# An earlier place for one batch's maxima in a latent-attention kernel: the order of work in the pair loop

## The chip, the cores and the metric

The kernel runs on one core of a Trainium2 chip. A core has five engines that run side by side: TensorE (PE in the profile; its weight loads are PEld), VectorE (DVE), ScalarE (ACT), GpSimd (POOL) and SyncE (SP, which here only issues DMAs). They wait for one another through semaphores. The metric is the device time of one execution in microseconds (us). The kernel before takes 814.68 us, the median of three runs (813.45 to 814.83).

## The reference

The reference is one block in three parts. The first is cross-attention of 64 latents on up to 1601 context rows plus the latents themselves, in each of 32 batches; it takes nearly all of the time. The second is a self-attention over the 64 latents, the third a quantised feed-forward layer.

```python
q = ln @ Wq                                   # ln: 64 latents x 128, per batch
k, v = split(concatenate((xn, ln)) @ Wkv)     # xn: context rows, normalised
sim = einsum('bhid,bhjd->bhij', q * scale, k) # 16 heads of 64
sim = where(mask_full, sim, -max)
attn = softmax(sim)
out = einsum('bhij,bhjd->bhid', attn, v) @ Wout
x = x + layernorm(out)
x = x + self_attention(layernorm(x))          # 16 heads of 8, with a slope bias
x = x + ffn(layernorm(x))                     # int8-like fake quantisation
```

The softmax needs, per head and latent, a maximum over all keys, which is subtracted before the exponential.

## The kernel before, in words

**Folding.** Keys are never formed. The queries are multiplied by the key weights, so that a "folded query" can be multiplied with the normalised context rows. Folded queries are made in three steps for a pair of batches, each in two halves: QP (latents times the query weights, lines 1376 to 1378), QC (times the key weights for the context, L1390) and QL (the same for the latents). Each has a high and a low 16-bit part: ACT copies the high part out of the bank, then DVE computes the low part (L1095 and L1903 for QP, L1103 and L1908 for QC, L1106 and L1912 for QL).

**Steps.** Here only the last 400 context rows of a batch differ in their mask and all earlier ones are masked out, so a flag that is read at run time picks the plan WINDOW, in which a batch has 8 steps. One body of the loop is one pair of batches: steps 0 to 7 belong to the even batch of pair i, steps 8 to 15 to the odd one. A step makes a bank of scores (L1435 to L1439), ACT turns them into two versions of the exponential (L1126 and L1117), POOL makes the low part (L861), and two steps later PE multiplies with the values (L1472). There are 16 bodies: body 0 and 1 written out, 2 to 14 in a loop of 13 turns, and body 15, which makes no queries.

**Jobs in between.** PE also makes the next work in advance, in "jobs" which alternate between two banks (jbank): T (transpose of the context rows, L1366), MAX (eight products of folded queries with all keys, only for the maximum, L1406 and L1407; DVE reduces each with L1916), MT (the eight maxima are negated by L1919, transposed by L1410, copied by L1923), QP, QC and QL. QP, T, MAX and MT take one bank each, QC and QL both banks. A job may start only when the bank it takes has been emptied, by DVE at last. The dictionary WINDOW gives each job its step: `ODD` the jobs of the odd batch of this body's pair, `NEXT` the queries of the next pair, `EVEN` the even batch of the next pair. At a step s, jobs at s are issued behind the step's scores and before its values, those at s+0.25 and s+0.5 behind the values, and the projections (L1552, L1569) and the self-attention of the pair before (`ST1`, `SC`, `ALIBI`, `SMAX`) behind those. Every engine walks the same table in its own program order. An instruction that waits holds all behind it on its engine.

**What the first MAX of the odd batch waits for.** The folded queries of QC are made one body ahead into a staging place (`arena`), and SP moves them to `qkc_h` and `qkc_l` by two DMAs (L636, L637). For the odd batch that move is the first thing that SP does in a body; it comes behind the DMA of line 668, which waits for DVE's reciprocal of the denominators (L1937, step 15 of the body before). The lines are these:

```python
if job.index == 0:
    pe.wait_ge(s_jobs_taken, plan.transposed_through(i, last, par))
    pe.wait_ge(s_lat_loaded[par], (b - par) * 8 + 16)
    if happened(b - 1):
        pe.wait_ge(s_qk_moved[par], (b - par) * 16)
```

`SMAX` is the reduction of the self-attention scores (L2028). POOL's subtraction (L929, `SHIFT`) waits for it.

Of the kernel before, what the change touches and what calls it, by code (L numbers as in the profile page):

```python
# [65 lines left out]
class Plan:  # L66
# [9 lines left out]
    def __init__(self, first, split, at):  # L76
# [19 lines left out]
        self.START = self.numbered(self.of_batch(0, at["START"]) + self.of_queries(at["START"]))  # L96
        odd, inner = self.of_batch(1, at["ODD"]), self.of_queries(at["NEXT"]) + self.of_batch(0, at["EVEN"])
        self.AHEAD = "AHEAD" in at
# [74 lines left out]
    START=dict(QP=[-3, -3], QC=[-2, -2], QL=[-1, -1], T=[0.5, 1.5, 2.5, 3.5], MAX=[11 + m // 3 + 0.5 * (m % 3 > 0) for m in range(32)], MT=23),  # L173
    ODD=dict(T=[0.5, 1.5, 2.5, 3.5], MAX=[11 + m // 3 + 0.5 * (m % 3 > 0) for m in range(32)], MT=23),
    NEXT=dict(QP=[5.5, 6.5], QC=[24.5, 26.5], QL=[33.5, 35.5]),
    EVEN=dict(T=[28.5, 29.5, 30.5, 31.5], MAX=[39 + m // 3 + 0.5 * (m % 3 > 0) for m in range(32)], MT=51), XV={8: (0, 3), 9: (3, 6), 10: (6, 9), 11: (9, 11), 12: (11, 13)},
    RDEN=(8, 8),
    MOVE=28, ST1=[10, 11, 14, 15], YN=[13, 17], XB=18, ST2=19, M0=21, P0=21, X1=22, X1B=23, M1=22, P1=23, XH=24, XHT=25, XHT_OUT=26, QKV=27, QKV_OUT=28,
    VBLK=29, KEXP=30, SC=34, ALIBI=[35, 37], SMAX=37, SHIFT=38, EXP=40, PT=[41, 43], PT_OUT=[42, 44],
# [1 line left out]
WINDOW = Plan(N - 400, ({0, 1, 2, 3, 4}, {0, 1, 2, 3, 4}), dict(  # L181
    STATS={4: (0, 4)}, AGGR=4, RSTD=5, XHAT=6, MASK=7,
    START=dict(QP=[-3, -3], QC=[-2, -2], QL=[-1, -1], T=[-2.5], MAX=[1, 1, 2, 2, 3, 3, 4, 4], MT=4.25),
    ODD=dict(T=[0], MAX=[2.5, 3, 3, 3.5, 4, 4, 4.5, 5], MT=6), AHEAD=[15.5],
    NEXT=dict(QP=[0, 0.5], QC=[1.5, 6.5], QL=[8.5, 9.5]),
    EVEN=dict(T=[7.5], MAX=[10.5, 11, 11, 11.5, 12, 12, 12.5, 13], MT=14.25), XV={2: (0, 4)},
    RDEN=(3, 7), MOVE=11, ST1=[4, 4, 6, 6], YN=[7, 7], XB=8, ST2=8, M0=9, P0=9, X1=10, X1B=20, M1=10, P1=11,
    XH=12, XHT=13, XHT_OUT=13, QKV=14, QKV_OUT=14, VBLK=15, KEXP=15.5, SC=17, ALIBI=[18, 20], SMAX=21, SHIFT=23, EXP=24,
    PT=[24, 25], PT_OUT=[24, 25], PV=26, CX=27, CXT=28, CXT_OUT=28, WO=29, X2=30, P2=31.5))


class Drain:
# [12 lines left out]
LAST_PAIR = Drain(True, dict(  # L205
    XB=1, DEN=0, ST1=[], RDEN=[1, 2], YN=[1, 2], ST2=[3, 4], M0=5, P0=5, X1=6, M1=6, P1=6, XH=7, XHT=7, XHT_OUT=7, QKV=8, QKV_OUT=8,
    KEXP=9, VBLK=10, SC=11, ALIBI=[12, 13], X1B=13, HALF_EXP=[12, 13], PT=[13, 14], PT_OUT=[14, 15],
# [5 lines left out]
def program(nc, x, ctx, mask, lnx_g, lnx_b, lnl_g, lnl_b, wq, wkv, wout, lno_g, lno_b,  # L213
            a_wq, a_bq, a_wk, a_bk, a_wv, a_bv, a_wo, a_bo, slopes, clip_x, clip_d, w_gate, w_up, w_down, out):
    es = ExitStack()
    with es:
# [1505 lines left out]
        def _(dve):  # L1722
# [234 lines left out]
            def second_norm(plan, p, s):  # L1957
                if s == plan.at["XH"]:
                    dve.wait_ge(s_rstd_a, p * 2 + 2)
                    centred(xh[:, :], x1[:, :], 1).then_inc(s_xh_ready, 1)  # L1960
# [231 lines left out]
```

## Time and profile before

| | |
|---|---|
| median of 3 runs | 814.68 us |
| the profiled execution | 815.53 us, span 813.8 us |
| PE busy | 749.8 us (92% of the span) |
| DVE busy | 597.5 us (73%) |
| ACT busy | 590.0 us (73%) |
| POOL busy | 543.7 us (67%) |
| mean granted clock of TensorE | 0.98 of full speed |

Times in the views are microseconds from the start of the span. In the views of single instructions a row gives the start, the time taken, the engine, the line and the tiles; several like instructions are merged (x3). Matmuls are pipelined: the difference of two starts tells what one costs, its own duration is longer. A bracket tells how long the engine sat idle and what ended it. The row `PEclk` of the page gives the granted clock of TensorE in tenths of full speed, in 40 slices.

### The profile page before, as it was taken

Reading aid. Unit: us, or ns where it says so; the run is one execution under the profiler, and the core shown is the slowest. Engines: PE = TensorE matmul, PEld = TensorE weight load, DVE = VectorE, ACT = ScalarE, POOL = GpSimd, SP = SyncE. Lnnn points to the kernel's source line nnn. Section 1 sums busy time; section 2 is a strip of 40 time slices with the busy share of each in tenths; the row PEclk is TensorE's granted clock in tenths of the full one; section 3 lists DMA queues with packets and bytes.
Section 4 is the critical chain, followed back from the end, with each engine's and each line's share of the span. In section 5 each row is a group of like instructions: output and inputs, shape, how many; then the busy total and the mean of one; then the engine's idle time right before and its main releaser. Section 6 shows DMA issues by size and latency. Waiting matters only on the chain.

```text
span 813.8 us, 22676 instructions
## 1 busy us (share of the span) xinstructions
PE 749.8 (92%) x7119; PEld 418.2 (51%) x7122; DVE 597.5 (73%) x1463; ACT 590.0 (73%) x1022; POOL 543.7 (67%) x712
## 2 busy tenths in 40 slices
PE   5698999999999999999999999999999999999666
PEld 3443544546555555555464555555555646455423
DVE  5877686676777777676767777776767676776677
ACT  5377777887878687878878686878787786866262
POOL 4366667676867768686868677686768686877122
PEclk9799999999999999999999999999999999999997
DMA  6302323121221202121211212021212122110001
GB/s 187 69 13 66 98 66 82 42 62 56 55 61 31 72 18 71 45 71 40 60 56 55 61 39 74 9 71 45 71 40 60 56 56 60 44 45 19 5 0 53
DMA packets 95822, 44.44 MB, mean 55 GB/s; under 512 B 66500, under 2 KB 87848, under 8 KB 95656
## 3 DMA queue, kind: packets, MB, share of 16 engines
q1 hardware_dynamic: 95728, 43.93, 19.5%
q8 instruction: 18, 0.29, 0.1%
q14 instruction: 20, 0.16, 0.1%
q10 hardware_dynamic: 56, 0.05, 0.0%
HBM read 24.20 MB, written 3.34 MB: 34 GB/s over the span
## 4 chain that ended last, share of the span: by engine, by line
PE 62%; DVE 17%; issue 11%; ACT 5%; POOL 3%; DVEq 1%; DMA 1%; ACTq 0%; POOLq 0%; SPq 0%
PE bank L1472 13%; PE bank L1552 7%; PE bank L1435 6%; PE bank L1439 5%; PE bank L1437 5%; PE bank L1390 4%; DVE mx L1916 3%; PE bank L1569 3%; DVE raw L1881 3%; PE bank L1407 3%; PE bank L1366 2%; PE bank L1587 2%; DVE qkl_l L1912 2%; PE bank L1406 2%; PE bank L1624 1%
## 5 line engine op out<-in xcount | busy, mean ns | idle before, releaser
L861 POOL TENSOR_TENSOR p<-arena,p 128x512 f16<-128x512 f32 x256 | 299.4, 1173 | 126.1 <-ACT arena L1117 124.6
L1126 ACT ACTIVATE p<-bank,maskbias 128x512 f16<-128x512 f32 x224 | 155.2, 693 | 103.5 <-PE bank L1439 101.4
L1472 PE MATMUL bank<-p,xv 128*128 128x512 f16 (+1 forms) x768 | 183.0, 381 | 1.3 <-POOL p L861 0.8
L1916 DVE TENSOR_REDUCE mx<-bank 128x1 f32<-128x464 f32 x256 | 154.0, 632 | 17.8 <-PE bank L1407 16.1
L1117 ACT ACTIVATE arena<-bank,maskbias 128x512 f32<-128x512 f32 x224 | 154.8, 691 | 0.0
L1472 PEld LDWEIGHTS bank<-p,xv 128*128 128x128 f16 (+1 forms) x768 | 58.5, 97 | 69.9 <-issue 23.0
L1912 DVE TENSOR_TENSOR qkl_l<-bank,qkl_h 128x512 f16<-128x512 f32 x64 | 41.1, 686 | 68.9 <-ACT qkl_h L1106 68.8
L1435 PE MATMUL bank<-qkc_h,xtT_h 128*128 128x512 f16 (+1 forms) x256 | 86.6, 389 | 0.0
L1437 PE MATMUL bank<-qkc_l,xtT_h 128*128 128x512 f16 (+1 forms) x256 | 85.0, 379 | 0.0
L1439 PE MATMUL bank<-qkc_h,xtT_l 128*128 128x512 f16 (+1 forms) x256 | 85.0, 379 | 0.0
L1407 PE MATMUL bank<-xtT_h,qkc_h 128*128 128x400 f16 x256 | 83.3, 338 | 0.0
L1881 DVE TENSOR_SCALAR raw<-raw,mv,rstd 128x128 f32<-128x128 f32 x128 | 72.7, 616 | 3.9 <-POOL rstd L870 2.0
L1908 DVE SCALAR_TENSOR_TENSOR arena<-bank,ident,arena 128x512 f16<-128x512 f32 x60 | 42.1, 743 | 27.6 <-ACT arena L1103 27.6
L1406 PEld LDWEIGHTS bank<-ltT,qkl_h 128*128 128x128 f16 x256 | 24.8, 97 | 71.0 <-DVE mx L1916 38.2
L1406 PE MATMUL bank<-ltT,qkl_h 128*128 128x64 f16 x256 | 50.9, 199 | 9.8 <-DVE mx L1916 5.1
L1552 PE MATMUL bank<-arena,wvF 128*64 128x128 f32 x960 | 59.0, 276 | 0.0
L1390 PE MATMUL bank<-arena,wk_h 64*128 64x128 f16 x1024 | 50.1, 217 | 5.3 <-DVE mT L1923 3.1
L1552 PEld LDWEIGHTS bank<-arena,wvF 128*64 128x64 f32 x960 | 51.8, 137 | 4.7 <-issue 3.3
L1390 PEld LDWEIGHTS bank<-arena,wk_h 64*128 64x128 f16 x1024 | 37.1, 94 | 32.8 <-DVE mT L1923 10.3
L1390 PE MATMUL bank<-arena,wk_l 64*128 64x128 f16 x512 | 46.1, 216 | 0.0
L1103 ACT ACTIVATE arena<-bank,ident 128x512 f16<-128x512 f32 x60 | 38.0, 685 | 8.3 <-PE bank L1390 8.3
L1903 DVE SCALAR_TENSOR_TENSOR arena<-bank,arena 128x512 f16<-128x512 f32 x32 | 22.0, 691 | 28.6 <-ACT arena L1095 28.6
(279 smaller groups left out, 1548.4 us busy)
## 6 DMA issues: line engine op xcount, KB each, us to landing
arena<-den_dram SPq DMA_DIRECT2D x62, 128.0 KB, 3.2
qkc_h<-arena SPq DMA_DIRECT2D x30, 256.0 KB, 2.4
qkc_l<-arena SPq DMA_DIRECT2D x30, 256.0 KB, 2.5
raw<-in_ctx SPq DMA_DIRECT2D x32, 192.0 KB, 2.4
lt<-lt_dram SPq DMA_DIRECT2D x60, 32.0 KB, 2.1
arena<-in_L_xattn_Wkv SPq DMA_DIRECT2D x1, 1024.0 KB, 7.5
raw<-in_ctx SPq DMA_DIRECT2D x64, 8.0 KB, 2.0
ltT_dram<-x_all SPq DMA_DIRECT2D x4, 256.0 KB, 3.0
```

Of the source, the lines that this page charges most:

```text
L861: g.tensor_tensor(p_halves[0:r, slot, 1, :], p_all[0:r, (plan.halves_made(0, k, t) - 1) % 2, :], p_halves[0:r, slot, 0, :], ALU.subtract). ...
L1117: a.activation(p_all[0:r, (plan.halves_made(0, k, t) - 1) % 2, :], sbank[t % SRING][0:r, :], ACT.Exp, bias=bias).then_inc(s_probs_ready, 1)
L1126: a.activation(p_halves[0:r, slot, 0, :], sbank[t % SRING][0:r, :], ACT.Exp, bias=bias)
L1390: op = mm(by_batch(both[odd])[:, :, to], w[rws, cl, c, :], q[rws, c, :].rearrange("p (k t) -> p k t", k=2), start=first, stop=final)
L1407: op = mm(bk[:, 0:rest], qkc_h[:, par, col], xtT_h[:, par, 512 * part:plan.KEYS], start=True, stop=True)
L1435: op = mm(dst, keys_h, q_h[:, col], start=True, stop=False)
L1437: op = mm(dst, keys_h, q_l[:, col], start=False, stop=False)
L1439: op = mm(dst, keys_l, q_h[:, col], start=False, stop=tile > 0)
L1472: op = mm(bk[:, :], halves_of[at, row, :], p_halves[at, slot, prob, :], start=tile < 2 and n == 0, stop=last and n == 2)
L1552: op = mm((one, two)[q // 2][E * odd:E * odd + E, (c % 4) * P:(c % 4) * P + P], wvF[:, cl, head:head + E], z[:, :, col:col + M], start=cl ...
L1881: op = v.tensor_scalar(raw[:, par, c, :], raw[:, par, c, :], mv[:, c, 0:1], rstd[:, c:c + 1], ALU.subtract, ALU.mult)
L1916: v.tensor_reduce(mx[:, hq_tile, part:part + 1], bk[:, 0:width], AX.X, ALU.max).then_inc(s_jobs_taken, 1)
```

## The change

Three entries of the table WINDOW change. No instruction is added or removed and none is computed otherwise; only the order on PE, ACT and DVE differs. On SP and POOL the order is the same.

```diff
-    ODD=dict(T=[0], MAX=[2.5, 3, 3, 3.5, 4, 4, 4.5, 5], MT=6), AHEAD=[15.5],
-    NEXT=dict(QP=[0, 0.5], QC=[1.5, 6.5], QL=[8.5, 9.5]),
+    ODD=dict(T=[0], MAX=[1, 1, 1.5, 1.5, 2.5, 2.5, 3, 3], MT=4.25), AHEAD=[15.5],
+    NEXT=dict(QP=[4.5, 5], QC=[5.5, 6.5], QL=[8.5, 9.5]),
-    ... ALIBI=[18, 20], SMAX=21, SHIFT=23, EXP=24,
+    ... ALIBI=[18, 20], SMAX=22, SHIFT=23, EXP=24,
```

On PE, in the turn of the loop, the odd batch's first two MAX jobs now stand directly behind the scores of step 1 (`qkc_h,xtT_h 64x512`), ahead of that step's values. These are rows of the difference:

```order
 L1435 MATMUL bank<-qkc_h,xtT_h 64x512 x2
 L1437 MATMUL bank<-qkc_l,xtT_h 64x512 x2
 L1439 MATMUL bank<-qkc_h,xtT_l 64x512 x2
+L1361 ISA
+L1395 REGISTER_ALU
+L1396 REGISTER_ALU
+L1398 REGISTER_ALU
+L1400 REGISTER_ALU
+L1406 MATMUL bank<-ltT,qkl_h 128x64
+L1407 MATMUL bank<-xtT_h,qkc_h 128x400
```

The ISA and REGISTER_ALU rows are the sequencer's: L1396 to L1400 compute the waits of the first MAX.

On ACT, in the turn of the loop of the kernel after, the two copies of QP and those of QC stand as follows, between the exponentials (L1126, L1117) of steps 4, 5 and 6; the words "waits" name the semaphores.

```order
185 L1117 ACTIVATE arena<-bank,maskbias 128x512 [waits p_lo]
186 L1090 ISA
187 L1095 ACTIVATE arena<-bank 128x512 [waits jobs_made]
188 L1119 REGISTER_ALU
189 L1126 ACTIVATE p<-bank,maskbias 128x512 [waits values_done,scores_ready]
190 L1116 REGISTER_ALU
191 L1117 ACTIVATE arena<-bank,maskbias 128x512 [waits p_lo]
192 L1090 REGISTER_ALU
193 L1095 ACTIVATE arena<-bank 128x512 [waits jobs_made]
194 L1090 REGISTER_ALU
195 L1100 ISA [waits jobs_made]
196 L1103 ACTIVATE arena<-bank,ident 128x2x256 [waits qk_moved1,qk_moved0]
```

The second copy of QP (row 193) follows both exponentials of step 5, and the copies of QC (from row 196) follow it at once. Before, the copies of QP stood at step 0 and those of QC at steps 1 and 6.

On DVE the self-attention maximum now stands behind the normalisation of the next context rows (L1881), and MT's copy (L1923) far ahead of both:

```order
-L1919 TENSOR_REDUCE negm<-mx 128x8
+L1879 REGISTER_ALU
+L1881 TENSOR_SCALAR raw<-raw,mv,rstd 128x128 x4
 L2027 ISA
 L2028 TENSOR_REDUCE smax<-arena 128x16
-L1895 REGISTER_ALU
-L1922 ISA
-L1923 CAST mT<-bank 8x128
-L1879 REGISTER_ALU
-L1881 TENSOR_SCALAR raw<-raw,mv,rstd 128x128 x4
```

## Rows read from the trace of the kernel before

**Rows 1.** The page: engines, granted clock by slices, chain of waits by engine.
```profile
PE 749.8 (92%) x7119; PEld 418.2 (51%) x7122; DVE 597.5 (73%) x1463; ACT 590.0 (73%) x1022; POOL 543.7 (67%) x712
PEclk9799999999999999999999999999999999999997
PE 62%; DVE 17%; issue 11%; ACT 5%; POOL 3%; DVEq 1%; DMA 1%; ACTq 0%; POOLq 0%; SPq 0%
```

**Rows 2.** Busy time by stretch: steps 0 to 7, then 8 to 15 of body 9.
```profile
core 0: us, PE busy (x) PEld busy (x) DVE busy (x) ACT busy (x) POOL busy (x), PEclk, DMA share, GB/s
438.94:461.34 22.40, 22.08 (x228) 12.17 (x228) 17.49 (x41) 15.81 (x27) 18.11 (x22) 1.00 0.24 65
461.34:483.51 22.17, 21.41 (x201) 12.17 (x201) 15.50 (x40) 18.79 (x34) 14.66 (x20) 1.00 0.14 41
```

**Rows 3.** Timeline of PE, start of body 9 (start, us, engine, line).
```profile
438.94 0.41 PE L1435 MATMUL bank<-qkl_h,ltT 128*64 128x512 f16 x2
...
440.04 0.23 PE L1376 MATMUL bank<-lq,wq_h 128*128 128x128 f16 x1
...
440.72 0.81 PE L1472 MATMUL bank<-p,xv 128*128 128x512 f16 x3
...
442.13 0.41 PE L1435 MATMUL bank<-qkc_h,xtT_h 128*64 128x512 f16 x2
...
442.90 0.82 PE L1472 MATMUL bank<-p,xv 128*128 128x512 f16 x3
443.81 0.29 PE L1390 MATMUL bank<-arena,wk_h 64*128 64x128 f16 x4
...
444.59 1.09 PE L1587 MATMUL bank<-arena,qT 64*64 64x512 f32 x8
```

**Rows 4.** Timeline of SP's queue, bodies 9 and 15.
```profile
440.06 0.53 SPq L636 DMA_DIRECT2D qkc_h<-arena  x1
440.63 0.60 SPq L637 DMA_DIRECT2D qkc_l<-arena  x1
...
707.78 0.59 SPq L637 DMA_DIRECT2D qkc_l<-arena  x1
```

**Rows 5.** The page, DMA issues: KB each, us to landing.
```profile
qkc_l<-arena SPq DMA_DIRECT2D x30, 256.0 KB, 2.5
```

**Rows 6.** Timeline of DVE in body 9.
```profile
438.95 0.20 DVE L1937 RECIPROCAL rcol<-rcol 128x8 f32<-128x8 f32 x1
...
442.99 0.69 DVE L1903 SCALAR_TENSOR_TENSOR arena<-bank,arena 128x512 f16<-128x512 f32 x1 [0.28 <-ACT arena L1095]
...
448.37 1.19 DVE L1916 TENSOR_REDUCE mx<-bank 128x1 f32<-128x464 f32 x2 [0.20 <-PE bank L1407]
...
455.37 1.22 DVE L2028 TENSOR_REDUCE smax<-arena 128x16 f32<-128x1024 f32 x1
...
458.57 1.40 DVE L1908 SCALAR_TENSOR_TENSOR arena<-bank,ident,arena 128x512 f16<-128x512 f32 x2
```

**Rows 7.** Timeline of ACT in body 9.
```profile
442.34 0.62 ACT L1095 ACTIVATE arena<-bank 128x512 f16<-128x512 f32 x1
...
454.38 0.69 ACT L1126 ACTIVATE p<-bank,maskbias 128x512 f16<-128x512 f32 x1 [2.77 <-PE bank L1439]
454.97 0.68 ACT L1117 ACTIVATE arena<-bank,maskbias 128x512 f32<-128x512 f32 x1
```

**Rows 8.** Timeline of PE, step 6 of body 9.
```profile
455.78 0.81 PE L1472 MATMUL bank<-p,xv 128*128 128x512 f16 x3
456.83 0.29 PE L1390 MATMUL bank<-arena,wk_h 64*128 64x128 f16 x4 [0.24 <-DVE mT L1923]
```

**Rows 9.** Timeline of PE, step 1 of body 15.
```profile
708.19 0.41 PE L1435 MATMUL bank<-qkc_h,xtT_h 128*64 128x512 f16 x2
```

**Rows 10.** Busy time by stretch, around the start of body 1.
```profile
77.50:80.90 3.40, 1.73 (x13) 0.78 (x12) 1.92 (x7) 0.69 (x2) 1.76 (x3) 1.00 0.03 2
80.90:84.30 3.40, 3.40 (x22) 2.20 (x21) 2.01 (x7) 2.11 (x4) 1.15 (x1) 0.50 0.73 223
```

More of the change, by code:

```diff
@@ L183 @@
     START=dict(QP=[-3, -3], QC=[-2, -2], QL=[-1, -1], T=[-2.5], MAX=[1, 1, 2, 2, 3, 3, 4, 4], MT=4.25),
-    ODD=dict(T=[0], MAX=[2.5, 3, 3, 3.5, 4, 4, 4.5, 5], MT=6), AHEAD=[15.5],
-    NEXT=dict(QP=[0, 0.5], QC=[1.5, 6.5], QL=[8.5, 9.5]),
+    ODD=dict(T=[0], MAX=[1, 1, 1.5, 1.5, 2.5, 2.5, 3, 3], MT=4.25), AHEAD=[15.5],
+    NEXT=dict(QP=[4.5, 5], QC=[5.5, 6.5], QL=[8.5, 9.5]),
     EVEN=dict(T=[7.5], MAX=[10.5, 11, 11, 11.5, 12, 12, 12.5, 13], MT=14.25), XV={2: (0, 4)},
     RDEN=(3, 7), MOVE=11, ST1=[4, 4, 6, 6], YN=[7, 7], XB=8, ST2=8, M0=9, P0=9, X1=10, X1B=20, M1=10, P1=11,
-    XH=12, XHT=13, XHT_OUT=13, QKV=14, QKV_OUT=14, VBLK=15, KEXP=15.5, SC=17, ALIBI=[18, 20], SMAX=21, SHIFT=23, EXP=24,
+    XH=12, XHT=13, XHT_OUT=13, QKV=14, QKV_OUT=14, VBLK=15, KEXP=15.5, SC=17, ALIBI=[18, 20], SMAX=22, SHIFT=23, EXP=24,
     PT=[24, 25], PT_OUT=[24, 25], PV=26, CX=27, CXT=28, CXT_OUT=28, WO=29, X2=30, P2=31.5))
```

## The prediction

> **What bounds the kernel now.** I read four views, in this order. The page comes first: PE is busy for 92% of the span, no other engine for over 73%, and the chain that ended last lies on PE for 62% [rows 1]. The granted clock is at its full level nearly throughout, so PE's work runs at full speed. The busy time by stretch comes next: one body takes 22.40 + 22.17 = 44.57 us, with PE busy for 43.5 us of it [rows 2]. The reader is to see that there is hardly an idle microsecond to win, while every wait that is put on PE shows in full. Then the timeline of PE through one body gives the distances between work and the next work, and the timelines of SP, DVE and ACT give what these must deliver in the meantime. Thirteen bodies (2 to 14) are alike; bodies 0, 1 and 15 I count apart.
>
> **What the change removes.** All instructions stay, so PE's work in a body stays as it is. Two waits can go. Before QC's second half PE waits: the values start at 455.78 and issue for 0.65 (three matmuls; those at 440.72 issue for as much, with QP's 0.7 and a small pause up to 442.13), but QC starts at 456.83, so 0.40 us are lost to MT's copy, which sat behind the 1.22 us of the self-attention maximum [rows 6, 8]. Before QC's first half it is 443.81 - 442.90 - 0.75 = 0.16 us [rows 3]. Together 0.56 us per body. This is all that the earlier place of MT and the later place of SMAX bring.
>
> **What it adds, first term: the moved queries come too late.** The first MAX of the odd batch needs the two DMAs of lines 636 and 637. In body 9 the second is issued at 440.63 and lands 2.5 us later, at 443.13 [rows 4, 5]. Before, this MAX stood at step 2.5, behind QC at 443.81 and more. Now it stands directly behind the scores of step 1. PE gets there so: the scores of step 0 take 438.94 to 440.04 = 1.10 us; QP's half, 440.04 to 440.72 = 0.68 us, is gone; values 0.65; the second half of QP is gone; the scores of step 1 take 442.13 to 442.90 = 0.77 us [rows 3]. That is 438.94 + 2.52 = 441.46. The wait is 443.13 - 441.46 = 1.7 us, and the values of step 1 stand behind it. Could the DMAs start sooner? They follow DVE's reciprocal at 438.95 and the DMA after it [rows 4, 6], and that is step 15's work, which is not changed. Bounds: 1.3 us (the distance in body 15, below) to 2.1 us if the landing comes 0.4 later beside other transfers. I take 1.7.
>
> **Second term: MAX jobs in fours.** Eight MAX jobs now stand in two groups of four, with the values or the scores in the middle. DVE needs 1.19 us for two reductions, 0.6 each [rows 6], and with two banks job n+2 waits for the reduction of job n. PE makes one in 0.2 us. In a group the four reductions take 2.4 us, and PE has 0.8 us of MAX work and 0.65 to 0.75 us between, so the fourth job waits about 0.4 us and the third about 0.1: 0.5 per group, 1.0 in all. Before, single jobs stood between scores and values and lost about 0.1 each time, 0.5 in all. Net 0.5 us; bounds 0 (DVE starts sooner than I think) and 1.0.
>
> **Third term: QP's second half right ahead of QC's first.** QC takes both banks, so it waits until DVE has emptied the bank of QP's second half. Before, QP's halves stood on both sides of the values at 440.72, QC behind a further 1.5 us of scores and values, and ACT was nearly free. Now the order on ACT is: both exponentials of step 5, then QP's copy. From the end of a step's scores ACT needs 0.2 to start, then 0.59 per exponential (454.38 to 454.97), so the copy starts 1.4 us after the scores [rows 7]. From the start of the copy (442.34) to QC (443.81) the old trace has 1.47 us, DVE's 0.69 within it [rows 3, 6, 7]. So QC can start 2.85 us after the scores; PE has 0.68 (QP) + 0.65 (values) = 1.33 us to do. Wait: 1.5 us. Lower bound 0.35: 1.47 + 0.2 less the 1.33, if ACT were free at once; upper 2.1, if ACT or DVE is late by one more operation of 0.6.
>
> **Fourth term: QC's second half one step behind its first.** Before, five steps lay between; now it is one. A QC starts at 456.83, and DVE has emptied its banks at 458.57 + 1.40 = 459.97, 3.14 us later, about 3.27 with the 0.13 that PE took to see it at 443.81 [rows 3, 6, 8]. PE has QC itself, 443.81 to 444.59 = 0.78, scores 0.65 and values 0.65, 2.08 in all. Wait: 1.2 us. Bounds 0.8 (DVE's second half overlapped better) and 1.8 (the exponentials or the normalisation get in between).
>
> The Trainium skill ("Perfetto Trace Analysis", Optimizing Tensor Performance, Matmuls) says that independent groups should rotate through different banks so that the emptying of one overlaps the next one's matmuls. By that rule alone the third and fourth term would be zero, since the jobs do alternate, and the sum would shrink by 2.7 us per body. The row at 456.83, which waits although it alternates, speaks against reading it so here [rows 8].
>
> **What costs nothing.** SMAX behind the normalisation: DVE's 1.22 us come later by some 2 us, and POOL's subtraction with it, which is needed by ACT in step 8; POOL is busy for 18.11 of 22.40 us there, so there is room [rows 2, 6]. If the cover were gone, ACT's exponential would be late by that 1.2 us and PE's transposes of step 8 with it; I keep 0.3 us for it in the range. The normalised rows are needed by T at 7.5; by then PE is itself 4 us late.
>
> **The sum.** Per body of the loop 1.7 + 0.5 + 1.5 + 1.2 - 0.56 = 4.3 us; 13 bodies 56 us. Bodies 0 and 1 lose 2.6 each (no first term: body 0 has no such DMA, and body 1 starts at half clock, [rows 10], so PE is no earlier than the landing): 5 us. Body 15 makes no queries: PE reaches the MAX at 708.19 + 0.77 = 708.96, the landing is at 707.78 + 2.5 = 710.28 [rows 4, 5, 9], so 1.3 + 0.5 = 2 us. Together 63 us on the profiled execution's 815.5 us: 878.4. The median lies 0.85 below the profiled one: 877.6, so 877 us. A change within 0.2% (1.6 us) could not be told from none.
>
> **Rivals.** (a) One of the three waits is hidden after all, most likely the QP or QC one, because DVE and ACT have idle time there. For it: DVE is busy 17.49 and ACT 15.81 of 22.40 us [rows 2]. Against it: the waits come from a chain in a row, not from load. With 1.2 to 1.5 us less in 15 bodies: 877 - 20 = 857 us.
> (b) The clock falls in addition. In 77.50 to 80.90 PE was busy for 1.73 of 3.40 us, and the next 3.40 us were granted 0.50 [rows 10], which is 1.2 of 2.4 GHz; they lost some 1.7 us. The change puts a gap of 1.7 us into each body. If every second body pays 1.7 us: 877 + 13 = 890 us, if each does: 900. The Trainium skill ("TensorE: Matmul & The Clock Gate", A second HAM failure mode: psum-queue depth-cycling) says that frequent short idling of PE between groups of matmuls while banks are cycled makes the clock swing between its levels; that is this rival. Against it: in the loop the old kernel's own short waits left the clock at 1.00 [rows 2].
> (c) Faster: the new waits are all hidden and only the 0.56 us plus the small waits around the maxima go, 0.9 us in each of 14 bodies: 815 - 13 = 802 us. This needs the queries to have landed 1.7 us sooner, by 441.46, which decides it, and nothing in the rows moves the reciprocal that they wait for.
> (d) No difference: the table's entries move jobs which wait for the same things anyway and the body stays at 44.6 us. PE's 43.5 us busy of 44.57 speak against it: there is no slack to take a wait [rows 2].
>
> **Chances.** The forecast 0.55, (a) 0.2, (b) 0.18, (c) 0.04, (d) 0.03. The forecast's own terms, all at their lower bounds (1.3 + 0 + 0.35 + 0.8 - 0.56 = 1.9 per body), would give 843; all at the upper (2.1 + 1.0 + 2.1 + 1.8 - 0.56 = 6.4) 910; they will not all err one way. A range of 850 to 896 holds the forecast, (a) and the milder half of (b). Slower by over 0.2%: 0.93; within: 0.03; faster: 0.04.
>
> **What the profile after would show.** Bodies of about 48.9 us instead of 44.57. On PE, behind the scores of step 1, idle time of 1.7 us ended by the DMA qkc_l<-arena; 1.5 us before QC's first half, ended by DVE's L1903; 1.2 before its second, ended by DVE's L1908; steps 8 to 15 still 22.2 us. The row of the granted clock at 1.00 in the loop decides against (b). I am wrong if the move of the queries is issued much earlier relative to step 0, if ACT has the copies done beside the exponentials, or if steps 0 to 7 take less than 24.5 us.

## The result and the profile after

| | before | after |
|---|---|---|
| median | 814.35 us (813.45 to 814.83, 4 runs) | 882.85 us (882.51 to 883.93, 4 runs) |
| the profiled execution | 815.5 us, span 813.8 | 882.6 us, span 880.9 |
| mean granted clock of TensorE | 0.98 | 0.98 |
| body 9, steps 0 to 7 and 8 to 15 | 22.40 + 22.17 = 44.57 us | 26.81 + 22.18 = 48.99 us |

The ratio is 1.085, its 95% interval 1.083 to 1.087: the kernel got 68.5 us slower. The forecast was 877 us with a range of 850 to 896. The page of the profile after, with the same rows as [rows 1]:

```profile
PE 757.6 (86%) x7122; PEld 413.5 (47%) x7122; DVE 597.2 (68%) x1463; ACT 591.7 (67%) x1022; POOL 541.5 (61%) x712
PEclk9799999999999999999999999999999999999898
PE 49%; DVE 22%; issue 13%; ACT 6%; DMA 5%; POOL 2%; SPq 1%; DVEq 1%; ACTq 0%; POOLq 0%
```

No engine has more to do: DVE, ACT and POOL are busy for the same microseconds within 0.5%. PE's busy time is modelled, and its 7.8 us more are no more work. What changed is the chain that ended last: PE's share of it falls from 62% to 49%, and DVE's rises from 17% to 22%, DMA's from 1% to 5%. That is how it looks when an order of work goes wrong: everybody is busy for a smaller share.

Busy time by stretch, steps 0 to 7 and 8 to 15 of body 9, beside [rows 2]; the last two rows are around a place in body 5 of which the explanation speaks:

```profile
core 0: us, PE busy (x) PEld busy (x) DVE busy (x) ACT busy (x) POOL busy (x), PEclk, DMA share, GB/s
477.98:504.79 26.81, 22.51 (x228) 11.92 (x227) 16.61 (x40) 15.89 (x27) 17.52 (x22) 1.00 0.20 54
504.79:526.97 22.18, 21.44 (x202) 12.19 (x201) 16.39 (x42) 18.80 (x34) 15.04 (x21) 1.00 0.14 41
283.90:287.30 3.40, 2.33 (x15) 1.07 (x19) 1.99 (x4) 1.36 (x3) 3.15 (x6) 0.88 0.63 169
287.30:290.70 3.40, 3.40 (x17) 0.49 (x9) 1.09 (x2) 0.41 (x1) 1.83 (x3) 0.62 0.04 2
```

All of the loss lies in the steps that the change touched, 4.41 us; the second half of the body is the same to 0.01. Where in the first half, the timeline of PE tells, beside [rows 3, 8]:

```profile
477.98 0.41 PE L1435 MATMUL bank<-qkl_h,ltT 128*64 128x512 f16 x2
...
482.32 0.20 PE L1406 MATMUL bank<-ltT,qkl_h 128*128 128x64 f16 x1 [1.64 <-DMA qkc_l<-arena]
...
483.46 0.33 PE L1407 MATMUL bank<-xtT_h,qkc_h 128*128 128x400 f16 x1
483.97 0.20 PE L1406 MATMUL bank<-ltT,qkl_h 128*128 128x64 f16 x1 [0.18 <-DVE mx L1916]
...
494.92 0.81 PE L1472 MATMUL bank<-p,xv 128*128 128x512 f16 x3
...
497.06 0.29 PE L1390 MATMUL bank<-arena,wk_h 64*128 64x128 f16 x4 [1.33 <-DVE arena L1903]
...
498.50 0.81 PE L1472 MATMUL bank<-p,xv 128*128 128x512 f16 x3
...
500.28 0.28 PE L1390 MATMUL bank<-arena,wk_h 64*128 64x128 f16 x4 [0.97 <-DVE arena L1908]
```

In this order: the first MAX waits for the moved queries, the last MAX of each group of four for the reduction two before it (a second one like it stands at 488.46), QC's first half for the emptied bank of QP, QC's second half for the emptied banks of its first. The bracket counts idle time only, and a matmul's end is modelled. So I take the cost of a wait from starts: start of the waiting instruction, less start of the one before it, less what that one takes to issue. For QC's first half that is 497.06 - 494.92 - 0.65 = 1.49 us.

SP's queue, beside [rows 4]. The move is issued as early in the body as before (1.69 us from its start, before too), and it lands 2.5 us later:

```profile
478.22 0.36 SPq L668 DMA_DIRECT2D den_dram<-rcol  x1
479.10 0.53 SPq L636 DMA_DIRECT2D qkc_h<-arena  x1
479.67 0.60 SPq L637 DMA_DIRECT2D qkc_l<-arena  x1
```

ACT and DVE around step 5, beside [rows 6, 7]. QP's copy (L1095) stands behind two exponentials. The split of QC's first half by L1908 ends at 498.82 + 1.41 = 500.23, 3.17 us after that half began, and QC's second half starts right behind it, at 500.28:

```profile
494.45 0.69 ACT L1126 ACTIVATE p<-bank,maskbias 128x512 f16<-128x512 f32 x1 [2.06 <-PE bank L1439]
495.04 0.68 ACT L1117 ACTIVATE arena<-bank,maskbias 128x512 f32<-128x512 f32 x1
495.61 0.60 ACT L1095 ACTIVATE arena<-bank 128x512 f16<-128x512 f32 x1
498.10 1.27 ACT L1103 ACTIVATE arena<-bank,ident 128x512 f16<-128x512 f32 x2 [1.89 <-PE bank L1390]
```

```profile
496.24 0.69 DVE L1903 SCALAR_TENSOR_TENSOR arena<-bank,arena 128x512 f16<-128x512 f32 x1 [2.29 <-ACT arena L1095]
498.82 1.41 DVE L1908 SCALAR_TENSOR_TENSOR arena<-bank,ident,arena 128x512 f16<-128x512 f32 x2 [1.89 <-ACT arena L1103]
500.14 1.95 DVE L1881 TENSOR_SCALAR raw<-raw,mv,rstd 128x128 f32<-128x128 f32 x4
```

ACT sat idle for 2.06 us ahead of the first of these rows, and for 1.89 ahead of the last; DVE for 2.29 and 1.89. Neither is short of time. ACT waits for PE, DVE for ACT, and PE for DVE.

### The profile page after: what moved, and what is told of

Same layout as the page of the kernel before. It is cut to its first block, busy times and chain, and to the rows that moved or that the text cites. A ratio compares the mean times of both kernels' runs of the same rounds, so it can differ in the third digit from the quotient of the medians.

```text
span 880.9 us, 22679 instructions
## 1 busy us (share of the span) xinstructions
PE 757.6 (86%) x7122; PEld 413.5 (47%) x7122; DVE 597.2 (68%) x1463; ACT 591.7 (67%) x1022; POOL 541.5 (61%) x712
## 4 chain that ended last, share of the span: by engine, by line
PE 49%; DVE 22%; issue 13%; ACT 6%; DMA 5%; POOL 2%; SPq 1%; DVEq 1%; ACTq 0%; POOLq 0%
PE bank L1472 9%; PE bank L1552 6%; DVE mx L1916 6%; PE bank L1435 5%; DMA qkc_l<-arena 4%; PE bank L1390 4%; PE bank L1439 3%; PE bank L1437 3%; PE bank L1569 3%; DVE raw L1881 3%; PE bank L1587 2%; PE bank L1407 2%; PE bank L1366 2%; PE bank L1406 2%; DVE qkl_l L1912 2%
## 5 line engine op out<-in xcount | busy, mean ns | idle before, releaser
L861 POOL TENSOR_TENSOR p<-arena,p 128x512 f16<-128x512 f32 x256 | 296.9, 1163 | 181.5 <-ACT arena L1117 179.8
L1126 ACT ACTIVATE p<-bank,maskbias 128x512 f16<-128x512 f32 x224 | 155.2, 693 | 115.5 <-PE bank L1439 113.3
L1916 DVE TENSOR_REDUCE mx<-bank 128x1 f32<-128x464 f32 x256 | 149.4, 633 | 68.6 <-PE bank L1407 68.5
L1117 ACT ACTIVATE arena<-bank,maskbias 128x512 f32<-128x512 f32 x224 | 155.1, 693 | 0.0
L1407 PE MATMUL bank<-xtT_h,qkc_h 128*128 128x400 f16 x256 | 81.3, 342 | 0.0
L1881 DVE TENSOR_SCALAR raw<-raw,mv,rstd 128x128 f32<-128x128 f32 x128 | 71.8, 612 | 3.9 <-POOL rstd L870 2.0
L1103 ACT ACTIVATE arena<-bank,ident 128x512 f16<-128x512 f32 x60 | 38.0, 684 | 38.0 <-PE bank L1390 38.0
L1908 DVE SCALAR_TENSOR_TENSOR arena<-bank,ident,arena 128x512 f16<-128x512 f32 x60 | 42.0, 741 | 28.0 <-ACT arena L1103 28.0
L1134 ACT ACTIVATE arena<-bank 128x512 f32<-128x512 f32 x64 | 38.3, 598 | 24.3 <-PE bank L1472 24.3
```

The lines of the kernel that those rows point to most:

```text
L861: g.tensor_tensor(p_halves[0:r, slot, 1, :], p_all[0:r, (plan.halves_made(0, k, t) - 1) % 2, :], p_halves[0:r, slot, 0, :], ALU.subtract). ...
L1117: a.activation(p_all[0:r, (plan.halves_made(0, k, t) - 1) % 2, :], sbank[t % SRING][0:r, :], ACT.Exp, bias=bias).then_inc(s_probs_ready, 1)
L1126: a.activation(p_halves[0:r, slot, 0, :], sbank[t % SRING][0:r, :], ACT.Exp, bias=bias)
L1407: op = mm(bk[:, 0:rest], qkc_h[:, par, col], xtT_h[:, par, 512 * part:plan.KEYS], start=True, stop=True)
L1881: op = v.tensor_scalar(raw[:, par, c, :], raw[:, par, c, :], mv[:, c, 0:1], rstd[:, c:c + 1], ALU.subtract, ALU.mult)
L1916: v.tensor_reduce(mx[:, hq_tile, part:part + 1], bk[:, 0:width], AX.X, ALU.max).then_inc(s_jobs_taken, 1)
```

## The experiments

Medians are set against runs of the kernel before on the same chip. "Body" is a whole turn of the loop, steps 0 to 7 first; where nothing else is said, the others are as in the changed kernel.

**The move of the queries sooner.** SP issues it ahead of the denominators' DMA, and takes that DMA's wait behind it.

```diff
                             move_queries(plan, i, 1)
+                            if plan is WINDOW:
+                                sp.wait_ge(s_rden_ready, b - 1)
+                                store_rden(par)
                             rden_spread(b - 2, par)
...
-                        if k == 1:
+                        if k == 1 and (plan is WHOLE or last):
                             rden_rows(b - 1, 1 - par, pair)
```

> The kernel after, with one difference: at the start of a body SP issues the two DMAs that move the odd batch's queries ahead of the denominators' DMA (line 668), which waits for DVE's reciprocal. Theory (the waits on PE add up, each with its own cause): the move is issued about 1.2 us sooner relative to step 0, so the wait of the first MAX falls from 1.64 to 0.5 us or less and nothing else moves; a body takes 47.8 us, the kernel 883 - 16 = 867 us. Rival (the waits stand for one another: PE runs into the next late engine): the body stays within 0.3 us of 48.98 and the kernel within 4 us of 883. Rival (the clock and traffic): the wait stays near 1.6 since the transfers take longer together.

Measured: 861.97 us, ratio 1.058 (1.056 to 1.060), body 25.49 + 22.16. PE's timeline (each line number is 6 higher here), a body from 418.57:

```profile
418.57 0.41 PE L1441 MATMUL bank<-qkl_h,ltT 128*64 128x512 f16 x2
...
421.58 0.20 PE L1412 MATMUL bank<-ltT,qkl_h 128*128 128x64 f16 x1 [0.33 <-DMA qkc_l<-arena]
```

```profile
418.40 0.54 SPq L636 DMA_DIRECT2D qkc_h<-arena  x1
418.99 0.60 SPq L637 DMA_DIRECT2D qkc_l<-arena  x1
419.70 0.53 SPq L671 DMA_DIRECT2D den_dram<-rcol  x1
```

The second DMA is issued 0.42 us after the body's start instead of 1.69, and the wait shrinks from 1.64 to 0.33. The body gives back 1.32 us, no less than the wait did (1.31). So nothing later was lurking behind this wait.

**The maxima one step later.**

```diff
-ODD=dict(T=[0], MAX=[1, 1, 1.5, 1.5, 2.5, 2.5, 3, 3], MT=4.25)
+ODD=dict(T=[0], MAX=[2, 2, 2.5, 2.5, 3, 3, 3.5, 3.5], MT=4.25)
```

> The kernel after, with the odd batch's maxima at steps 2, 2, 2.5, 2.5, 3, 3, 3.5, 3.5 instead of 1, 1, 1.5, 1.5, 2.5, 2.5, 3, 3; the rest of the change stays. Theory of added waits: the queries have landed long before, the wait of 1.64 us is gone, the fours still lose 0.7; the waits before QC stay at 1.33 and 0.97 in the idle column. Body 47.3 us, kernel 883 - 25 = 858 us (14 bodies). Rival (one wait stands for the other): body unchanged within 0.3 us.

Measured: 860.12 us, 1.056 (1.054 to 1.057), body 25.69 + 22.17, 1.12 less. The DMA wait is gone altogether; a new one of 0.27 us appears, ahead of values:

```profile
418.41 0.82 PE L1472 MATMUL bank<-p,xv 128*128 128x512 f16 x3 [0.27 <-POOL arena L903]
```

This is the same cause, taken away from the other side: the DMAs stay, their reader comes later. The time is near the expected 858 us, but a body gives back less than the 1.68 us expected. The new wait takes a part of it, and the maxima in their new places make small pauses for the scores and values around them.

**The maxima not in fours.**

```diff
-MAX=[1, 1, 1.5, 1.5, 2.5, 2.5, 3, 3]
+MAX=[1, 1, 1.5, 2, 2.5, 3, 3, 3.5]
```

> The kernel after, with the maxima at 1, 1, 1.5, 2, 2.5, 3, 3, 3.5 instead of two groups of four. Theory: each group's last product waited 0.34 us for a bank, because DVE reduces one in 0.6 us; with scores or values between, this goes. Body 48.98 - 0.7 = 48.3 us, kernel 873 us. Rival (the wait is hidden in the wait before QC that follows, since that one ends by ACT's and DVE's chain): within 3 us of 883.

Measured: 871.74 us, 1.071 (1.070 to 1.073), body 26.19 + 22.18, 0.62 less. The two waits of 0.18 for L1916 are gone, the other three stay. By starts, the last product of a group was 0.34 us late, so the two groups lost 2 x 0.34 = 0.68 us.

**QP one step sooner.**

```diff
-NEXT=dict(QP=[4.5, 5], QC=[5.5, 6.5], QL=[8.5, 9.5])
+NEXT=dict(QP=[3.5, 4.5], QC=[5.5, 6.5], QL=[8.5, 9.5])
```

> The kernel after, with QP at steps 3.5 and 4.5 instead of 4.5 and 5, so that the projection of 1.9 us and the scores lie between QP's second half and QC. Theory of added waits: the wait before QC's first half (1.49 us) goes, that before the second half (1.13 us) and that for the DMA (1.72) stay; body 47.5 us, kernel 883 - 22 = 861 us. Rival (DVE and ACT are as a whole too late in steps 4 to 6, so QC has to wait for them anyway): less than 0.5 us per body, kernel over 875 us.

Measured: 863.52 us, 1.059 (1.058 to 1.061), body 25.60 + 22.17, 1.22 less. The wait before QC's first half is gone. It gives back less than 1.49 for two reasons that the starts show: QC without any wait comes 0.74 us behind the start of the values here, not 0.65, so the wait itself was 1.40; and the transpose of the maxima (L1410), which now stands in front of QP's second half, costs 0.28 us instead of 0.11. The others stay as they were:

```profile
424.12 0.20 PE L1406 MATMUL bank<-ltT,qkl_h 128*128 128x64 f16 x1 [1.64 <-DMA qkc_l<-arena]
...
440.88 0.28 PE L1390 MATMUL bank<-arena,wk_h 64*128 64x128 f16 x4 [0.98 <-DVE arena L1908]
```

**QC's halves further apart as well.**

```diff
-NEXT=dict(QP=[4.5, 5], QC=[5.5, 6.5], QL=[8.5, 9.5])
+NEXT=dict(QP=[3.5, 4.5], QC=[5, 6.5], QL=[8.5, 9.5])
```

> The kernel after, with QP at 3.5 and 4.5 as in the run before and, in addition, QC's first half at 5 instead of 5.5, ahead of the values of step 5 instead of behind them. Theory: 0.65 us more work lies between QC's halves, so the wait of 1.13 us before the second falls to about 0.5; the wait before the first stays away, since the projection and the scores cover it. Body 47.75 - 0.65 = 47.1 us, kernel 863.5 - 9 = 854 us. Rival (the banks' emptying is bound by how early ACT gets to it, behind the exponentials of step 5): the wait before the first half comes back by 0.65 and the time stays at 863.

Measured: 858.24 us, 1.054 (1.052 to 1.055), body 25.17 + 22.16. Half a step more between the halves gives 0.42 us beyond the run before it, and the wait is 0.55 instead of 0.98. That is less than expected (0.65 us, 854 us): the values that now lie between are 0.66 us of work, but the round trip has grown with them. From the start of QC's first half to the start of its second it was 3.23 us, now it is 3.45, because ACT's copy of the first half (L1103) now has to wait for both exponentials of step 5, which in the run before were done by then, and starts 1.26 us after the half began instead of 1.04. So a part of the rival came true: how early ACT gets to the banks counts too.

```profile
435.44 0.28 PE L1390 MATMUL bank<-arena,wk_h 64*128 64x128 f16 x4 [0.55 <-DVE arena L1908]
```

**The move, QP and QC together.** The edit of the first run and that of the one just told.

> The kernel after, with all three repairs: the moves sooner on SP, QP at 3.5 and 4.5, QC at 5 and 6.5. Theory of added waits: the gains add, 1.32 + 1.22 + 0.65 = 3.2 us per body; what stays are 0.34 for the DMA, 0.7 for the maxima in fours and 0.5 between QC's halves. Body 45.8 us, kernel 883 - 21 - 19 - 9 = 834 us. Rival (waits stand for one another): over 845 us.

Measured: 839.32 us, 1.031 (1.029 to 1.033). Steps 0 to 7 of a body:

```profile
407.06:430.93 23.87, 22.62 (x230) 11.87 (x229) 16.61 (x40) 15.89 (x27) 17.53 (x22) 1.00 0.22 61
```

That is 2.94 us less than 26.81. The first two alone gave 1.32 and 1.22, the third 0.42 on top of the second: 2.96 together. The gains add, so none of these waits hides another. The expected 834 us were missed mostly because they count 0.65 for QC's distance, and not the 0.42 just told.

**QP back at the start of the body.**

```diff
-NEXT=dict(QP=[4.5, 5], QC=[5.5, 6.5], QL=[8.5, 9.5])
+NEXT=dict(QP=[0, 0.5], QC=[5.5, 6.5], QL=[8.5, 9.5])
```

> The kernel after, with QP back at 0 and 0.5 and everything else as changed. Theory of added waits: QP's 1.36 us then stand where PE waits for the moved queries, so that wait falls from 1.64 to about 0.3, and the wait before QC's first half goes (its banks were emptied long before); the wait between QC's halves (0.97) and the fours stay. Body 48.98 - 1.36 - 1.49 = 46.1 us, kernel 883 - 40 = 843 us. Rival (the maxima's early place alone costs most of it): over 860 us.

Measured: 843.5 us, 1.036 (1.034 to 1.037), body 24.09 + 22.15, 2.73 less. One job in its old place takes one wait away and most of another: it gives QC its distance, and its own work on PE, 0.68 + 0.76 = 1.44 us, stands in front of the first MAX while the DMA is on its way. The wait there is 0.32 us where it was 1.64. The wait between QC's halves stays at 0.98.

```profile
414.29 0.20 PE L1406 MATMUL bank<-ltT,qkl_h 128*128 128x64 f16 x1 [0.32 <-DMA qkc_l<-arena]
```

**The self-attention maximum back.** The change with `SMAX=21` instead of 22.

> The kernel after, with SMAX back at 21. Theory: in the kernel after, MT's copy is early anyway and DVE is idle for 1.89 us before QC's low part, so the place of the self-attention maximum costs and brings nothing: 883 us, within 2. Rival (part of the loss is that SMAX delays POOL's subtraction and through it step 8): 3 us or more are won back.

Measured: 881.85 us, 1.083 (1.081 to 1.086), body 26.81 + 22.15. No difference from the changed kernel: there MT stands at 4.25, so its copy has long been made when L2028 comes.

**The self-attention maximum alone.** The kernel before with one number changed.

```diff
-XH=12, ..., ALIBI=[18, 20], SMAX=21, SHIFT=23, EXP=24,
+XH=12, ..., ALIBI=[18, 20], SMAX=22, SHIFT=23, EXP=24,
```

> The kernel before, with nothing but SMAX at 22 instead of 21: the self-attention maximum of 1.22 us no longer stands before MT's copy. Theory: the 0.40 us that PE waits before QC's second half goes in 15 bodies, everything behind it has room; body 44.2 us, kernel 814.4 - 6 = 808.5 us. Rival (the later SMAX delays POOL's subtraction and PE's transposes in step 8, or the normalisation's follower T at 7.5): no gain or a loss of up to 0.5 us per body, 814 to 821 us.

Measured: 811.52 us (810.29 to 812.31), ratio 0.995 (0.994 to 0.997), so 3.3 us faster than the kernel before, where 6 had been expected. A body:

```profile
437.25:459.39 22.14, 22.05 (x230) 12.08 (x229) 16.74 (x40) 15.86 (x27) 17.45 (x22) 1.00 0.25 65
459.39:481.55 22.16, 21.41 (x201) 12.16 (x200) 16.56 (x42) 18.75 (x34) 15.20 (x21) 1.00 0.14 41
```

```profile
454.40 0.28 DVE L1923 CAST mT<-bank 8x128 f16<-8x128 f32 x1 [0.66 <-DMA xtT_h<-onesrow]
454.61 2.28 DVE L1881 TENSOR_SCALAR raw<-raw,mv,rstd 128x128 f32<-128x128 f32 x4
456.81 1.21 DVE L2028 TENSOR_REDUCE smax<-arena 128x16 f32<-128x1024 f32 x1
```

MT's copy now stands ahead of the 1.21 us of L2028, and PE's wait of 0.24 us for it [rows 8] is gone. The body is 0.27 us shorter, 13 x 0.27 = 3.5 us. The expected 0.40 was 1.05 us from the values to QC less 0.65 for the values; with nothing to wait for it is 0.74 here, so 0.31 could be won, and 0.04 of it goes again at T (0.57 us from its start to the next scores instead of 0.53). (The bracket puts DVE's 0.66 us ahead of the copy down to a DMA. The copy's input is a bank of PE, which transposes what DVE made at 453.57; I read those 0.66 us as the way over PE.)

**Two tries to get more on top of it.** In the kernel before, the last wait of a body is 0.43 us before T, for the normalised rows. Both tries keep `SMAX=22`. First: the statistics, the root, the normalisation and the mask of these rows one step sooner. Second, against another wait, of 0.21 us ahead of the even batch's seventh maximum: that maximum half a step later, when its bank has long been free.

```diff
-STATS={4: (0, 4)}, AGGR=4, RSTD=5, XHAT=6, MASK=7,
+STATS={3: (0, 4)}, AGGR=3, RSTD=4, XHAT=5, MASK=6,
```

> The kernel before, with SMAX at 22 and the statistics of the next context rows, their root, normalisation and mask one step sooner (STATS 3, AGGR 3, RSTD 4, XHAT 5, MASK 6). Theory: PE's wait of 0.43 us (0.6 with the sequencer's part) before T at 15.5 comes from the normalisation, which starts only when POOL's root is ready at step 13; one step sooner takes the wait away. Body 44.30 - 0.5 = 43.8 us, kernel 811.5 - 7 = 804.5 us. Rival (the normalisation of 2 us then stands ahead of the last reductions of the maxima on DVE, and MT or the denominators are late): the wait moves elsewhere, 811 us or more.

Measured: 846.64 us, 1.039 (1.037 to 1.041), body 24.39 + 22.31. The expectation failed. The wait before T is gone, but PE's timeline has three new ones:

```profile
469.13 0.20 PE L1406 MATMUL bank<-ltT,qkl_h 128*128 128x64 f16 x1 [1.23 <-DVE mx L1916]
...
476.21 0.28 PE L1390 MATMUL bank<-arena,wk_h 64*128 64x128 f16 x4 [0.97 <-DVE mT L1923]
...
495.92 0.20 PE L1406 MATMUL bank<-ltT,qkl_h 128*128 128x64 f16 x1 [1.07 <-DVE mx L1916]
```

DVE works in a row: the statistics (0.86 us) and the normalisation (1.95 us) now stand ahead of reductions and of a copy that free banks. 

```profile
466.87 0.86 DVE L1868 BATCH_NORM_STATS2 st<-raw 128x6 f32<-128x128 f32 x4
...
474.01 1.95 DVE L1881 TENSOR_SCALAR raw<-raw,mv,rstd 128x128 f32<-128x128 f32 x4
475.89 0.27 DVE L1923 CAST mT<-bank 8x128 f16<-8x128 f32 x1
```

```diff
-EVEN=dict(T=[7.5], MAX=[10.5, 11, 11, 11.5, 12, 12, 12.5, 13], MT=14.25)
+EVEN=dict(T=[7.5], MAX=[10.5, 11, 11, 11.5, 12, 12, 13, 13], MT=14.25)
```

> The kernel before with SMAX at 22 and the even batch's seventh maximum at 13 instead of 12.5, ahead of which PE waits 0.21 us for a bank in each body. Theory: at 13 the bank has been free for long, so the wait goes: body 44.3 - 0.25 = 44.05 us, kernel 811.5 - 3.5 = 808 us. Rival (the last reductions then end later, and with them the normalisation and the wait before T at 15.5): no gain or a loss of 0.3 us per body, 811.5 to 816 us.

Measured: 816.76 us (12 runs), 1.003 (1.002 to 1.004), body 22.42 + 22.36, where `SMAX=22` alone has 22.14 + 22.16. The expectation failed here too, and the rival came true. The wait of 0.21 us is gone, but the wait before T grew from 0.43 to 0.93 us, and another one came, which this run has in 15 bodies and the run with `SMAX=22` alone in 3: the first scores of a body wait 0.21 us for a DMA issued behind MT's copy, which now comes later.

```profile
438.50 0.66 PE L1366 MATMUL bank<-ident,raw 128*128 128x128 f32 x4 [0.93 <-POOL raw L873]
...
440.14 0.40 PE L1443 MATMUL bank<-mrow,onesrow 1*64 1x512 f16 x2 [0.21 <-DMA qkc_h<-mT]
```

So `SMAX=22` alone remains the best version found, and it beats both kernels.

## Why the prediction was right, step by step

**The sum of a body.** The forecast was 4.3 us, measured 4.41. Term by term, from starts:

| term | forecast | by starts, after against before | given back when taken away |
|---|---|---|---|
| first MAX waits for the moved queries | 1.7 | 482.32 - 480.29 - 0.31 = 1.72 | 1.32 (rest of 0.33 stays) |
| MAX in fours | 0.5 net | 2.53 - 2.01 = 0.52 | 0.62 |
| QP, then QC | 1.5 | 1.49 | 1.22 |
| QC, then QC | 1.2 | 500.28 - 498.50 - 0.65 = 1.13 | 0.42 of it, by half a step |
| waits of before that go | -0.56 | -0.40 - 0.23 = -0.63 | 0.27 by SMAX alone |

The last row is the 1.05 us from the values to QC's second half less 0.65, and the 0.91 from the values to QC's first half, where the values of step 1 now take 0.68. The middle column adds up to 4.23. The 0.18 that is missing from 4.41 lies in small pauses with no bracket, 0.10 of it at the values of step 0 (0.75 us where they took 0.65 in front of QP). The last column is the test of the causes: the second and third wait vanish when only their own cause is taken away, the first shrinks by about as much as the DMAs come sooner (1.31 for 1.27), and three edits together give the sum of their gains. For the fourth only a part was tried, which gave 0.42 us for 0.66 us of work; QC's halves a further step apart were not run.

**The maxima in fours, looked at closely.** I set 1.0 us against 0.5 of before. From the start of each MAX job to the start of what follows it, the eight jobs take 2.53 us in the body after and 2.01 in the body before, against 8 x 0.20 = 1.60 for jobs that lose nothing. So 0.93 against 0.41, and the net of 0.52 is what was forecast. Inside a group it is not as I had it. The third job waits for nothing, the fourth is 0.34 us late, and a group's last job costs 0.30 instead of 0.20 with other work behind it. In the body before, one job was late by 0.14 us:

```profile
450.14 0.19 PE L1406 MATMUL bank<-ltT,qkl_h 128*128 128x64 f16 x1
...
450.48 0.20 PE L1406 MATMUL bank<-ltT,qkl_h 128*128 128x64 f16 x1
```

The variant with the maxima not in fours agrees: its eight jobs take 2.08 us.

**What was to cost nothing.** The later maximum costs nothing: putting it back in the changed kernel changes nothing. In the kernel before, it alone wins 0.27 us in a body. The 0.40 that I gave to the wait before QC's second half [rows 8] was 0.09 too much, since QC comes 0.74 us behind the start of the values even when nothing holds it. The change's own gain was there, but the change brought it twice (MT sooner, SMAX later), and buried it under four waits.

**The rest of the program.** Span after less span before is 67.1 us, where 63 were forecast. By the starts of the bodies: 0.5 ahead of body 0, then 3.2, 1.6 and 5.9 in bodies 0, 1 and 2, 54.4 in bodies 3 to 14, 1.6 in body 15. The forecast for these was 0, 2.6, 2.6, 4.3, 51.6 and 2.0.
- Body 0 waits for L1916 before four maxima, 0.54, 0.18, 1.31 and 0.18 us; the first and the third have no like in the loop. I had not worked out a size of its own for it, and 2.6 was the loop's figure less its first term.
- Body 1: the half clock of [rows 10] doesn't come in this execution. That gives back about 1.7 us, while the DMA wait that I had set at 0 is there, with 0.88 us. The forecast for this body is near only because these two errors go opposite ways.
- Body 2 has a longer DMA wait than the others, 2.63 us. The move was issued at 132.63 and PE goes on at 136.86, 4.2 us later instead of 2.65. Every variant in which the first MAX keeps its place has a longer wait here than in its other bodies. Other transfers running beside it would be a ready guess, but the rows do not bear it out. From the body's start, the two stretches of body 2 have a DMA share of 0.45 and 0.57, and the same two stretches of body 9, where the move is on time, have 0.37 and 0.60. Why it lands late in body 2 stays open.

```profile
136.86 0.23 PE L1406 MATMUL bank<-ltT,qkl_h 128*128 128x64 f16 x1 [2.63 <-DMA qkc_l<-arena]
```

Busy time by stretch, body 2 and then body 9:

```profile
131.30:134.70 3.40, 2.70 (x18) 0.76 (x17) 0.69 (x1) 3.33 (x5) 2.31 (x3) 1.00 0.45 154
134.70:138.10 3.40, 1.24 (x6) 0.64 (x7) 0.64 (x2) 1.46 (x3) 2.20 (x2) 0.73 0.57 145
478.04:481.44 3.40, 2.63 (x18) 0.77 (x17) 1.43 (x6) 2.76 (x5) 3.40 (x5) 1.00 0.37 130
481.44:484.84 3.40, 2.35 (x19) 0.95 (x19) 2.12 (x4) 1.34 (x3) 3.15 (x6) 1.00 0.60 166
```

- The clock. In bodies 2 and 5 of this execution the granted clock fell to half, the 1.2 GHz level, behind the DMA wait. In body 5 the two stretches of 3.40 us shown above were granted 0.88 and 0.62 on average. With levels of 1.0 and 0.5, that is 0.8 and 2.6 us at half, and body 5 took 1.6 us longer than its neighbours.

**Rival (b)** was therefore not wrong in kind: it came, but in 2 of the 14 bodies from 1 on, and cost about 3 us of the 68.5 by an estimate: 1.6 in body 5, and about 1.4 in body 2, where PE was back at work for some 2.8 us of the half clock. The Trainium skill ("TensorE: Matmul & The Clock Gate", A second HAM failure mode: psum-queue depth-cycling) lets one expect swings of the clock from frequent short idling. Here the loop idles for 1.64, 1.33 and 0.97 us in every body and was at 1.00 in 12 of 14. The measurement decides: a hazard, not the cost. The runs point to the wait at the DMA as what brings it about, but do not show it. The five kernels that keep this wait in full (the change itself, QP sooner, QC apart, SMAX back, the fours split) have waits of 2.36 to 2.79 us in body 2, and in each of them the clock falls once right there. The ones that shorten or remove it (the move sooner, the maxima one step later, all three edits, QP back at 0) have at most 1.62 us in body 2 and no fall there. Two further falls, in body 5 here and in body 14 of the run with QC apart, came in bodies with the usual wait. And a fall at the start of body 1, as in [rows 10], also came with QP sooner, with QP back at 0, with SMAX alone and with the even maximum later, so it needs none of the new waits. Each is one execution, so this is an observation and not a count.

**Rival (a)**, one wait hidden by idle time of ACT and DVE, fell: all are there. The idle time is there too, 2.06 and 1.89 us in the rows of ACT, but ahead of the work, not beside it. The rule of the Trainium skill that was weighed ("Perfetto Trace Analysis", Optimizing Tensor Performance, Matmuls), independent groups through different banks so that emptying overlaps, does not save these jobs, since QC takes both banks of the rotation. Distance does it: with QP sooner, so that the projection and the scores lie in between, the wait goes to nothing. **Rivals (c) and (d)** needed the queries landed by 2.5 us after the body's start, or slack on PE; they land at 4.2, and there was none.

## What to carry to other kernels

When one engine is busy nearly all the time, as PE is here for 92% of the span, a table that only reorders work is judged by distances: for each pair of producer and consumer, PE's work between them against the time of the round trip (here 2.8 us from the scores to QC, through two exponentials, a copy and a split; 3.2 us for QC through ACT and DVE; 2.5 us for a DMA behind its issue). A move that shortens a distance below its round trip costs the difference in every turn, and here the differences added. The round trip is no constant: with its first half moved closer behind a step's scores, QC had to wait for that step's exponentials on ACT, and the round trip went from 3.23 to 3.45 us. Split such a change and time each number by itself: the one useful number of this one was worth 0.5% alone.

## What was not expected of the hardware

The normalisation of four tiles (L1881, 128x128 each) took 1.95 us in the loop before and after, but 2.28 us with `SMAX=22` alone, where it starts 0.4 us sooner in the body (17.36 instead of 17.76 us from its start). The instructions and their shapes are the same; what they run beside is not. The traces show what decides: POOL's subtraction L861, and where in it an instruction starts. With `SMAX=22` alone:

```profile
454.04 1.16 POOL L861 TENSOR_TENSOR p<-arena,p 128x512 f16<-128x512 f32 x1 [1.38 <-ACT arena L1117]
455.53 1.28 POOL L861 TENSOR_TENSOR p<-arena,p 128x512 f16<-128x512 f32 x1 [0.34 <-ACT arena L1117]
```

The first of the four starts at 454.61, while the first L861 is running, and takes 0.67 us instead of 0.33; it ends 0.08 us after that L861. The last starts during the second L861, takes 1.18 us, and ends 0.08 us after it. The two between, with no L861 at their start, take 0.33 and 0.34. In the kernel before, the first of the four starts in the last 0.2 us of an L861 and takes its 0.33, and only the last is held, with 1.18 us. It is the same in all 13 traces, 128 of these instructions in each: one that starts while no L861 is running takes 0.32 to 0.35 us, and one that starts while an L861 is running never ends earlier than 0.08 us after it and takes up to 1.24. So I read the extra time as DVE being held by POOL: the instruction has started, so no semaphore holds it, and it counts as busy meanwhile. What in the chip holds it, no run shows. It doesn't explain why the gain was 0.27 us instead of 0.40; that is the 0.74 us told above.

Where a release by DMA is short of time, its cost is not constant over the program: the same 256 KB move had PE waiting until 2.65 us after its issue in body 9 and 4.2 us in body 2.
